# Half 0's second layer with tokens on the partitions, its norm's power ahead of weight pieces, and half 1's masks on GpSimd

## The chip, the core and the metric

The kernel runs on one core of a Trainium2 chip. In the profile PE is TensorE (PEld its weight loads), DVE is VectorE, ACT is ScalarE, POOL is GpSimd, and SP is SyncE, whose queue issues all DMAs. The metric is the device time of one execution in microseconds, the median of 3 runs.

## The reference, cut to what matters

There are 1024 tokens of 256 features. Two blocks follow each other, each with a residual. In the first, one of four experts is picked for each token by its id, and all three weights of an expert are the same matrix `ctx`:

```
e   = min(id // 3125, 3)                      # expert of each token
xn  = layernorm(x)
z   = xn @ ctx[e].T ;  h = silu(z) * z
x1  = x + h @ ctx[e].T                        # second product of the same matrices
```

The second block is a mixture of 16 experts of width 96 with a shared expert of width 96:

```
xn     = layernorm(x1)
score  = sigmoid(xn @ router.T) ; top 4 of (score + bias), weights normalised to their sum
y      = shared(xn) + sum over the 4 of weight * ((silu(xn @ gate.T) * (xn @ up.T)) @ down.T)
out    = x1 + y
```

## The kernel before, in words

Everything is in fp32. Each matrix product is made of three matmuls: every operand is split into a rounded high part and a low part (the rest), and high*high, low*high and high*low are added up in PSUM. High parts are casts, mostly by ScalarE (`high_part`, `x_high`, `hidden_high`, `hid_high`); low parts are subtractions, those of the weights by GpSimd (`low_part`), the others by VectorE.

The tokens go in two halves of 512. Data are feature-major (features on the 128 partitions, tokens along the free dimension), except for the layer norms, which want tokens on the partitions. So before a norm the tile is turned, then normalised, then turned back by TensorE (`norm_transposes`).

The first block is a list of "mixes" `(layer, half, feature half)`. `mix(n)` computes all four experts for 128 output features and 512 tokens: 24 matmuls, into four PSUM banks of a ring of six (`ring_order`, `wait_ring_read`). ScalarE copies expert 0 out (`first_z`), and VectorE overwrites it with the experts 1 to 3 where a mask says so (`pick`, masks `beyond` made by `thresholds`). `x1_transposes` turns the result of half 0 for its second norm: statistics (`tile_stats`, `layer_norm_vars`), then a power -0.5 on GpSimd (`rstd_of`), then shift and scaling (`layer_norm_apply` on VectorE, `apply_norm` on ScalarE; `BY_VECTOR` says who takes which tile).

The second block is a loop over 26 items g, each a chunk of 128 hidden features of one half: gate and up products (`gate_or_up`, 12 matmuls), silu on ScalarE, `product` with the combine weights, `hidden_2`, the split (`hid_high`, `hid_low`), and two items later the `down` product (6 matmuls). The combine weights come out of the router chain (`turn_logits`, `mark_best`, `normalise_scores`), go to DRAM (`write_rows`) and are read back spread over the partitions (`spread_rows`).

The order on each engine is written out by hand. The engines meet only in semaphores. The weights come in 15 pieces through four slots of `stage`: 0 to 3 are `ctx`, 4, 5, 8, 9, 11, 12 and 14 gate and up, 6, 7, 10 and 13 down; a slot is loaded again when both parts of its piece have been cut.

## Time and profile before

| | us |
|---|---|
| median of 3 runs | 169.52 (169.2 to 170.2) |
| the profiled execution | 169.34 |
| its span, first to last instruction | 167.2 |
| PE busy | 162.5 (97%) |
| DVE busy | 114.5 (68%) |
| ACT busy | 68.7 (41%) |
| POOL busy | 37.2 (22%) |

The granted TensorE clock was 1.00 over the whole span, which is the higher of its two levels, 2.4 GHz. A busy share is of the span. Times in the rows below are from the start of the span. In the timeline a matmul's duration (0.40 us for 512 columns) is longer than the distance to the next one, since matmuls are pipelined; the distance is what it costs.

### The profile page before, as it was taken

To read this page: it belongs to the slowest core of one execution; us is meant where nothing else is said; L and a number is where in the kernel's file an instruction comes from. 1 tells how busy PE (TensorE), PEld (TensorE's weight loads), DVE (VectorE), ACT (ScalarE), POOL (GpSimd) and SP (SyncE) were. 2 spreads that over 40 slices of the span, in tenths; PEclk is the share of its full clock that TensorE was granted. 3 is DMA by queue.
4 is the path that set the end of the run, shared out by engine and by line. 5 is a ranking of instruction groups with operands and counts; after the bars stand their busy time and mean duration, and the time that the engine had idled before them with its cause. 6 is when DMAs were issued, how large, how long until landed. Compare 5 with 4: busy or idle time off the path is not lost.

```text
span 167.2 us, 2186 instructions
## 1 busy us (share of the span) xinstructions
PE 162.5 (97%) x705; PEld 128.9 (77%) x705; DVE 114.5 (68%) x237; ACT 68.7 (41%) x116; POOL 37.2 (22%) x36
## 2 busy tenths in 40 slices
PE   7999999999999999999999999999999999999992
PEld 2788888888778888888888878888888888888880
DVE  1889999666957998779986744967714444444462
ACT  3654342831359134536734538452222222222210
POOL 1384000656241045556970000000000000000000
PEclk9999999999999999999999999999999999999999
DMA  5891380164304065987225400025441112200003
GB/s 172 275 408 44 107 291 0 21 206 161 115 4 127 16 205 192 219 240 211 67 61 163 153 0 4 1 103 165 173 141 67 63 63 63 65 0 0 4 0 125
DMA packets 12199, 18.78 MB, mean 112 GB/s; under 512 B 3772, under 2 KB 6044, under 8 KB 12060
## 3 DMA queue, kind: packets, MB, share of 16 engines
q1 hardware_dynamic: 12188, 18.64, 34.9%
q8 instruction: 6, 0.10, 0.2%
q14 instruction: 5, 0.04, 0.1%
HBM read 16.39 MB, written 2.24 MB: 111 GB/s over the span
## 4 chain that ended last, share of the span: by engine, by line
PE 95%; DMA 2%; DVE 1%; DVEq 0%; issue 0%
PE bank L1030 23%; PE bank L1131 15%; PE bank L1129 13%; PE bank L1130 13%; PE bank L1149 7%; PE bank L1152 7%; PE bank L1150 7%; DMA first<-first_d 2%; PE bank L998 1%; PE bank L1071 1%; PE bank L1065 1%; PE bank L1126 1%; PE bank L1125 1%; PE bank L987 1%; PE bank L1078 1%; PE bank L1060 1%
## 5 line engine op out<-in xcount | busy, mean ns | idle before, releaser
L1131 PE MATMUL bank<-xn_lo,gu_hi 128*128 128x512 f32 (+1 forms) x104 | 41.1, 395 | 0.0
L1129 PE MATMUL bank<-xn_hi,gu_lo 128*128 128x512 f32 x96 | 38.0, 396 | 0.0
L1130 PE MATMUL bank<-xn_hi,gu_hi 128*128 128x512 f32 x96 | 38.0, 396 | 0.0
L599 ACT ACTIVATE h_hi<-hid 128x512 fp32r<-128x512 f32 (+1 forms) x26 | 16.4, 632 | 45.6 <-DVE hid L860 45.6
L865 DVE TENSOR_TENSOR h_lo<-hid,h_hi 128x512 fp32r<-128x512 f32 (+1 forms) x26 | 18.0, 691 | 14.9 <-ACT h_hi L599 14.9
L1131 PEld LDWEIGHTS bank<-xn_lo,gu_hi 128*128 128x128 f32 (+1 forms) x104 | 19.4, 187 | 4.9
L589 ACT ACTIVATE act_sb<-bank 128x512 f32<-128x512 f32 (+1 forms) x26 | 15.4, 592 | 17.5 <-PE bank L1131 17.4
L472 POOL TENSOR_TENSOR gu_lo<-stage,gu_hi 128x512 fp32r<-128x512 f32 x12 | 17.2, 1457 | 21.7 <-ACT gu_hi L504 16.3
L1129 PEld LDWEIGHTS bank<-xn_hi,gu_lo 128*128 128x128 f32 x96 | 18.0, 188 | 4.4
L1130 PEld LDWEIGHTS bank<-xn_hi,gu_hi 128*128 128x128 f32 x96 | 18.0, 188 | 4.3
L749 DVE COPY_PREDICATED prod<-beyond,bank 128x512 f32<-128x512 uint8 x24 | 17.6, 737 | 5.1 <-PE bank L1030 4.4
L1149 PE MATMUL bank<-h_hi,wd_lo 128*128 128x512 f32 (+1 forms) x52 | 20.6, 396 | 0.0
L1150 PE MATMUL bank<-h_hi,wd_hi 128*128 128x512 f32 (+1 forms) x52 | 20.6, 395 | 0.0
L1152 PE MATMUL bank<-h_lo,wd_hi 128*128 128x512 f32 (+1 forms) x52 | 20.5, 395 | 0.0
L860 DVE TENSOR_TENSOR hid<-prod,bank 128x512 f32<-128x512 f32 x24 | 16.5, 688 | 2.0
L847 DVE TENSOR_TENSOR prod<-act_sb,ids 128x512 f32<-128x512 f32 x12 | 9.6, 796 | 8.6 <-ACT act_sb L589 8.6
L847 DVE TENSOR_TENSOR prod<-act_sb,first 128x512 f32<-128x512 f32 x12 | 10.0, 832 | 6.3 <-ACT act_sb L589 5.7
L1030 PE MATMUL bank<-h_hi,ctx_hi 128*128 128x512 f32 x32 | 12.7, 398 | 0.0
L1030 PE MATMUL bank<-h_lo,ctx_hi 128*128 128x512 f32 x32 | 12.7, 395 | 0.0
L1030 PE MATMUL bank<-h_hi,ctx_lo 128*128 128x512 f32 x32 | 12.7, 395 | 0.0
L1152 PEld LDWEIGHTS bank<-h_lo,wd_hi 128*128 128x128 f32 (+1 forms) x52 | 9.8, 188 | 2.4
L1150 PEld LDWEIGHTS bank<-h_hi,wd_hi 128*128 128x128 f32 (+1 forms) x52 | 9.8, 188 | 2.3
(102 smaller groups left out, 213.2 us busy)
## 6 DMA issues: line engine op xcount, KB each, us to landing
stage<-gu_d SPq DMA_DIRECT2D x6, 512.0 KB, 3.9
stage<-wd_d SPq DMA_DIRECT2D x3, 512.0 KB, 4.3
first<-comb_d SPq DMA_DIRECT2D x8, 192.0 KB, 2.9
ids<-comb_d SPq DMA_DIRECT2D x8, 192.0 KB, 3.3
stage<-ctx_d SPq DMA_DIRECT2D x4, 256.0 KB, 6.0
xt<-xt_d SPq DMA_DIRECT2D x1, 1024.0 KB, 9.9
first<-comb_d SPq DMA_DIRECT2D x8, 128.0 KB, 3.0
ids<-comb_d SPq DMA_DIRECT2D x8, 128.0 KB, 2.9
```

The source lines that it names most:

```text
L472: ins = nc.gpsimd.tensor_tensor(lo[:, s], st[:, s], hi[:, s].bitcast(F32), ALU.subtract)
L749: nc.vector.copy_predicated(prod[:, n % 2], beyond[:, e - 1, h * HALF:(h + 1) * HALF], ring_bank("z", n, e)[:]).then_inc(z_picked, 1)
L847: nc.vector.tensor_tensor(prod[:, g % 2], act_sb[:, g % 2], rows, ALU.mult).then_inc(prod_done, 1)
L860: nc.vector.tensor_tensor(hid[0:w, g % 2], src, up_bank(g)[0:w, :], ALU.mult).then_inc(hid_done, 1)
L865: nc.vector.tensor_tensor(h_lo[0:w, slot[g]], hid[0:w, g % 2], h_hi[0:w, slot[g]].bitcast(F32), ALU.subtract).then_inc(hlo_done, 1)
L1030: return nc.tensor.matmul(ring_bank("z", n, e)[:], (ctx_hi, ctx_lo)[a][:, m, e, k], parts[k][b], start=start, stop=stop)
L1129: nc.tensor.matmul(out[:], gu_lo[:, cols], xn_hi[:, h, k], start=(k == 0), stop=False)
L1130: nc.tensor.matmul(out[:], gu_hi[:, cols], xn_hi[:, h, k], start=False, stop=False)
L1131: ins = nc.tensor.matmul(out[0:rows, :], gu_hi[:, wide], xn_lo[:, h, k], start=False, stop=(k == KC - 1))
L1149: nc.tensor.matmul(acc[k][:], wd_lo[0:w, c, cols], hi, start=(c == 0), stop=False)
L1150: nc.tensor.matmul(acc[k][:], wd_hi[0:w, c, cols], hi, start=False, stop=False)
L1152: ins = nc.tensor.matmul(acc[k][:], wd_hi[0:w, c, cols], lo, start=False, stop=(c == ITEMS - 1))
```

## The change

In the second product of half 0, tokens and weights change places. `row_mix` takes the hidden tile h as the stationary operand, 128 tokens at a time, and the weights of two experts as the moving one (512 columns: two experts by 256 features). The result is token-major, so it needs no transposes ahead of the norm, and `x1_transposes` is gone. The picks are made per tile of 128 tokens (`row_z`, `pick_rows`, with masks `beyond_rows` from `row_thresholds`), the residual x is added from a token-major copy that is loaded into the place of half 0 in `xt` (`x_rows_d`), and the statistics read it there. Tile t holds the tokens 128 q + 32 t + i on the partitions 32 q + i; `hidden` writes h in that order, and the "n2" transposes of half 0 write it back in the natural one. Since the output needs x1 feature-major, VectorE turns it later in blocks of 32x32 (`turn_x0`, behind items 8 and 9), and SyncE writes it to DRAM and reads it back (`write_x0` and `read_x0`, at items 12 and 13). The two mixes `(2, 0, m)` leave the list; mixes 5, 6 and 7 become 3, 4 and 5.

The masks of half 1 are made by GpSimd (`late_thresholds`) behind low part 3. GpSimd's powers move too: those of the first two norms stand between low parts, that of half 0's second norm stands behind low part 5, ahead of pieces 6 and 7; these two now stand behind the wait for `xlo_done`, with piece 8. Half 1's first mix `(1, 1, 1)` is picked as a whole between the variance and the norm.

```diff
-        ring_order = [("z", n, e) for n in range(7) for e in range(E1)]
-        ring_order += [("gate", 0, 0), ("up", 0, 0)] + [("z", 7, e) for e in range(E1)]
+            count = (HALVES * KC if what == "n2" else 0) + h * KC + k + 1
+            eng.wait_ge(xhi_done, max(count, KC))
+            eng.wait_ge(xlo_done, count)
+
+        ring_order = [("z", n, e) for n in range(3) for e in range(E1)]
+        ring_order += [("rows", t, pair) for t in range(TT) for pair in range(2)]
+        ring_order += [("z", n, e) for n in (3, 4) for e in range(E1)]
+        ring_order += [("gate", 0, 0), ("up", 0, 0)] + [("z", 5, e) for e in range(E1)]
...
+            if b >= KC:
+                return tile[:, at]
+            order = "p (b t j) -> p b t j" if tile is hid else "p (t b j) -> p b t j"
+            return tile[:, at].rearrange(order, t=TT, j=LANES)
...
-        mixes = [(1, 0, 0), (1, 0, 1), (1, 1, 0), (2, 0, 0), (2, 0, 1), (1, 1, 1), (2, 1, 0), (2, 1, 1)]
+        mixes = [(1, 0, 0), (1, 0, 1), (1, 1, 0), (1, 1, 1), (2, 1, 0), (2, 1, 1)]
...
+            return x1_rows[:, t] if n == HALVES else x[:, n % HALVES * TT + t]
...
-            sp.dma_start(xt[:], xt_d).then_inc(xt_in, 16)
+            sp.dma_start(xt[:, :, HALF:], xt_d[:, :, HALF:]).then_inc(xt_in, 16)
+            sp.dma_start(id_rows[:], id_rows_d).then_inc(id_rows_in, 16)
+            sp.dma_start(xt[:, :, 0:HALF], x_rows_d).then_inc(x_rows_in, 16)
...
+            def read_x0():
+                sp.wait_ge(x0_out, QUARTERS * 16)
+                rows = turn_d.rearrange("q k i n -> q i k n")
+                for q in range(QUARTERS):
+                    sp.dma_start(xt[q * LANES:(q + 1) * LANES, :, 0:HALF], rows[q]).then_inc(x0_back, 16)
...
+            def late_thresholds():
+
+                pool.wait_ge(ids_in, 16)
+                for e in range(1, E1):
+                    nc.gpsimd.tensor_scalar(beyond[:, e - 1, HALF:], ids[:, HALF:], float(e * PER_EXPERT), None,
+                                            ALU.is_ge).then_inc(late_masked, 1)
...
-            for n in range(E1):
+            low_part(0)
+            low_part(1)
+            rstd_of(0)
+            low_part(2)
+            rstd_of(1)
+            low_part(3)
+            late_thresholds()
+            for n in range(E1, E1 + 2):
                 low_part(n)
-            rstd_of(0)
-            rstd_of(1)
-            for n in range(E1, E1 + 3):
-                low_part(n)
-            pool.wait_ge(x1_done, KC)
-            low_part(E1 + 3)
             rstd_of(2)
             pool.wait_ge(xlo_done, (HALVES + 1) * KC)
-            for n in range(E1 + 4, early_pieces + 4):
+            for n in range(E1 + 2, early_pieces + 4):
...
+            def row_z(t):
+
+                act.wait_ge(row_done, 2 * t + 1)
+                nc.scalar.activation(x1_rows[:, t], ring_bank("rows", t, 0)[:, 0:D], ACT.Copy).then_inc(row_first, 1)
...
             first_z(2)
-            first_z(3)
+            row_z(0)
             silu_z(2)
             hidden_high(2)
+            row_z(1)
             high_part(4)
             high_part(5)
+            row_z(2)
             high_part(6)
-            first_z(4)
+            row_z(3)
             high_part(7)
             high_part(8)
             router_low_rows()
-            first_z(5)
-            silu_z(5)
+            first_z(3)
+            silu_z(3)
...
+            def pick_rows(t, experts=range(1, E1)):
+
+                dve.wait_ge(row_first, t + 1)
+                dve.wait_ge(rows_masked, E1 - 1)
+                for e in experts:
+                    dve.wait_ge(row_done, 2 * t + e // 2 + 1)
+                    if e > 1:
+                        dve.wait_ge(row_picked, t * (E1 - 1) + e - 1)
+                    z = ring_bank("rows", t, e // 2)[:, e % 2 * D:(e % 2 + 1) * D]
+                    nc.vector.copy_predicated(x1_rows[:, t], beyond_rows[:, e - 1, t:t + 1].to_broadcast([P, D]),
+                                              z).then_inc(row_picked, 1)
+
+            def add_rows(t):
+
+                dve.wait_ge(row_picked, (t + 1) * (E1 - 1))
+                dve.wait_ge(x_rows_in, 16)
+                residual = xt[:, t * D // HALF, t * D % HALF:][:, 0:D]
+                nc.vector.tensor_tensor(x1_rows[:, t], x1_rows[:, t], residual, ALU.add).then_inc(row_added, 1)
+
+            def turn_x0(first):
+
+                dve.wait_ge(xn_out, QUARTERS * 16)
+                blocks = x[:, TT:].rearrange("p t d -> p (t d)").rearrange("p (q k t i) -> p t k q i", k=KC, t=TT, i=LANES)
+                for t in range(first, first + 2):
+                    for k in range(KC):
+                        ins = nc.vector.transpose(blocks[:, t, k],
+                                                  x1_rows[:, t, k * P:(k + 1) * P].rearrange("p (q i) -> p q i", i=LANES))
+                    ins.then_inc(x0_turned, 1)
...
-            masked.append(thresholds(1))
-            pick(2, masked[1])
-            pick(3, masked[0], [1])
+            row_thresholds()
+            pick(2, masked[0])
+            pick_rows(0, [1])
             hidden_product(2)
-            pick(3, masked[0], [2])
+            pick_rows(0, [2])
             hidden_low(2)
-            pick(3, masked[0], [3])
-            add_block_1(3)
-            pick(4, masked[0])
-            add_block_1(4)
-            pick(5, masked[1], [1])
-            for t in range(TT):
-                tile_stats(2, t)
+            pick_rows(0, [3])
+            add_rows(0)
+            for t in range(1, TT):
+                tile_stats(2, t - 1)
+                pick_rows(t)
+                add_rows(t)
+            tile_stats(2, TT - 1)
             layer_norm_vars(2)
-            pick(5, masked[1], [2, 3])
+            pick(3, masked[0])
             layer_norm_apply(2)
...
-            pick(6, masked[1], [1])
+            pick(4, masked[0], [1])
...
+            pick(4, masked[0], [2])
             normalise_scores(0, mark_best(0))
-            pick(6, masked[1], [3])
-            add_block_1(6)
-            pick(7, masked[1], [1])
+            pick(4, masked[0], [3])
+            add_block_1(4)
...
+                if X0_TURN <= g < X0_TURN + TT // 2:
+                    turn_x0((g - X0_TURN) * 2)
...
+                        if n == HALVES:
+                            out = banks[k][:].rearrange("p (b t j) -> p t b j", t=TT, j=LANES)[:, t]
...
+            def row_mix():
+
+                hi, lo = ([w[:, b].rearrange("p (t c) -> p t c", c=P) for b in range(KC)] for w in (h_hi, h_lo))
+
+                def moving(w, pair, k):
+                    return w[:, :, 2 * pair:2 * pair + 2, k].rearrange("p m e f -> p e m f")
+
+                for t in range(TT):
+                    for pair in range(2):
+                        wait_ring_read(pe, "rows", t, pair)
+                        out = ring_bank("rows", t, pair)[:].rearrange("p (e m f) -> p e m f", e=2, m=KC)
+                        for k in range(KC):
+                            if t == 0 and pair == 0:
+                                pe.wait_ge(h1_high, k + 1)
+                            nc.tensor.matmul(out, hi[k][:, t], moving(ctx_hi, pair, k), start=(k == 0), stop=False)
+                            nc.tensor.matmul(out, hi[k][:, t], moving(ctx_lo, pair, k), start=False, stop=False)
+                            if t == 0 and pair == 0:
+                                pe.wait_ge(h1_done, k + 1)
+                            ins = nc.tensor.matmul(out, lo[k][:, t], moving(ctx_hi, pair, k), start=False, stop=(k == KC - 1))
+                        ins.then_inc(row_done, 1)
...
-            for n in range(2, 5):
-                mix(n)
-            mix(5, {1: lambda: (x1_transposes(0, 0), x1_transposes(0, 1))})
-            mix(6, features=[0])
+            mix(2)
+            row_mix()
+            mix(3)
+            mix(4, features=[0])
             norm_transposes("n2", 2, 0)
-            mix(6, experts=[0, 1], features=[1])
+            mix(4, experts=[0, 1], features=[1])
             gate_or_up(0, False)
             gate_or_up(0, True)
-            mix(6, experts=[2, 3], features=[1])
-            mix(7)
+            mix(4, experts=[2, 3], features=[1])
+            mix(5)
```

The first place is GpSimd's order from the first low part on, to the second pair of gate-and-up pieces. `ctx_lo`, `gu_lo` and `wd_lo` are low parts of weights, `deviation` and `rstd` are powers. Before:

```order
L468 TENSOR_TENSOR ctx_lo<-stage,ctx_hi 128x512 x4
L478 TENSOR_TENSOR deviation<-vareps,power 128x4
L478 TENSOR_TENSOR rstd<-vareps,power 128x4
L468 TENSOR_TENSOR gu_lo<-stage,gu_hi 128x448
L472 TENSOR_TENSOR gu_lo<-stage,gu_hi 128x512 x2
L468 TENSOR_TENSOR wd_lo<-stage,wd_hi 96x256
L472 TENSOR_TENSOR wd_lo<-stage,wd_hi 128x512 x2
L478 TENSOR_TENSOR rstd<-vareps,power 128x4
L472 TENSOR_TENSOR gu_lo<-stage,gu_hi 128x512 x4
```

Now (`beyond` are the masks of half 1):

```order
L505 TENSOR_TENSOR ctx_lo<-stage,ctx_hi 128x512 x2
L522 TENSOR_TENSOR deviation<-vareps,power 128x4
L505 TENSOR_TENSOR ctx_lo<-stage,ctx_hi 128x512
L522 TENSOR_TENSOR rstd<-vareps,power 128x4
L505 TENSOR_TENSOR ctx_lo<-stage,ctx_hi 128x512
L516 TENSOR_SCALAR beyond<-ids 128x512 x3
L505 TENSOR_TENSOR gu_lo<-stage,gu_hi 128x448
L509 TENSOR_TENSOR gu_lo<-stage,gu_hi 128x512 x2
L522 TENSOR_TENSOR rstd<-vareps,power 128x4
L505 TENSOR_TENSOR wd_lo<-stage,wd_hi 96x256
L509 TENSOR_TENSOR wd_lo<-stage,wd_hi 128x512 x2
L509 TENSOR_TENSOR gu_lo<-stage,gu_hi 128x512 x4
```

Three compares stand behind the last `ctx_lo`, the powers `deviation` and the first `rstd` each stand one low part earlier than the end of the four, and the first down pieces (`wd_lo`, 96x256 and 128x512 x2) have moved behind the later `rstd`.

The second place is VectorE's order from the end of half 0's second product to the norm of it. `prod` and `bank` are picks of a mix, `stats`, `meanvar`, `vareps` and `shift` belong to the norm, `xn` is its result. Before:

```order
L749 COPY_PREDICATED prod<-beyond,bank 128x512
L777 TENSOR_TENSOR xt<-prod,xt 128x512
L749 COPY_PREDICATED prod<-beyond,bank 128x512 x3
L777 TENSOR_TENSOR xt<-prod,xt 128x512
L749 COPY_PREDICATED prod<-beyond,bank 128x512
L670 BN_STATS stats<-bank 128x6 x4
L676 BN_AGGR meanvar<-stats 128x2 x4
L678 TENSOR_SCALAR vareps<-meanvar 128x4
L749 COPY_PREDICATED prod<-beyond,bank 128x512 x2
L713 SCALAR_TENSOR_TENSOR shift<-meanvar,rstd 128x4
```

Now (`x_rows` is x1, token-major):

```order
L835 TENSOR_TENSOR x_rows<-x_rows,xt 128x256
L727 BN_STATS stats<-x_rows 128x6
L827 COPY_PREDICATED x_rows<-beyond_rows,bank 128x256 x3
L835 TENSOR_TENSOR x_rows<-x_rows,xt 128x256
L727 BN_STATS stats<-x_rows 128x6
L733 BN_AGGR meanvar<-stats 128x2 x4
L735 TENSOR_SCALAR vareps<-meanvar 128x4
L808 COPY_PREDICATED prod<-beyond,bank 128x512 x3
L770 SCALAR_TENSOR_TENSOR shift<-meanvar,rstd 128x4
L778 TENSOR_SCALAR xn<-x_rows,meanvar,rstd 128x256 x2
```

The statistics of a tile stand between the tiles' picks and no longer in one group behind transposes, and all three picks of the mix of half 1 stand between the variance and the shift, where there were two.

## Rows read from the trace of the kernel before

**Rows 1.** The page: busy time, share and instructions by engine; the chain by engine.
```profile
PE 162.5 (97%) x705; PEld 128.9 (77%) x705; DVE 114.5 (68%) x237; ACT 68.7 (41%) x116; POOL 37.2 (22%) x36
...
PE 95%; DMA 2%; DVE 1%; DVEq 0%; issue 0%
```

**Rows 2.** Timeline of PE from 38.9 us: start, duration, engine, line, operation, output<-input, count.
```profile
38.90 1.04 PE L1010 MATMUL bank<-first,xt 128*128 128x128 f32 x8
39.69 0.48 PE L1030 MATMUL bank<-xn_hi,ctx_hi 128*128 128x512 f32 x1
40.01 0.39 PE L1030 MATMUL bank<-xn_hi,ctx_lo 128*128 128x512 f32 x1
40.24 0.39 PE L1030 MATMUL bank<-xn_lo,ctx_hi 128*128 128x512 f32 x1
```

**Rows 3.** Timeline of PE and its weight loads, start of mix 1 and "n1" transposes.
```profile
12.61 0.19 PEld L1030 LDWEIGHTS bank<-xn_hi,ctx_hi 128*128 128x128 f32 x1
...
15.64 1.03 PE L987 MATMUL bank<-first,xn 128*128 128x128 f32 x8
```

**Rows 4.** Timeline of POOL, DVE and ACT, 8.8 to 15.9 us.
```profile
8.79 3.80 POOL L468 TENSOR_TENSOR ctx_lo<-stage,ctx_hi 128x512 fp32r<-128x512 f32 x3 [1.01 <-ACT ctx_hi L504]
9.46 0.65 DVE L678 TENSOR_SCALAR vareps<-meanvar 128x4 f32<-128x4 f32 x1
...
12.55 1.18 POOL L478 TENSOR_TENSOR deviation<-vareps,power 128x4 f32<-128x4 f32 x1
13.53 1.03 POOL L478 TENSOR_TENSOR rstd<-vareps,power 128x4 f32<-128x4 f32 x1
...
14.59 0.16 DVE L713 SCALAR_TENSOR_TENSOR shift<-meanvar,rstd 128x4 f32<-128x4 f32 x1
14.67 0.73 DVE L721 TENSOR_SCALAR xn<-first,meanvar,rstd 128x256 f32<-128x256 f32 x2
14.79 1.09 ACT L542 ACTIVATE xn<-first,shift,rstd 128x256 f32<-128x256 f32 x2 [4.30 <-DVE shift L713]
```

**Rows 5.** Timeline of POOL and DVE, the second norm of half 1.
```profile
80.67 2.55 POOL L472 TENSOR_TENSOR wd_lo<-stage,wd_hi 128x512 fp32r<-128x512 f32 x2
81.06 0.92 DVE L713 SCALAR_TENSOR_TENSOR shift<-meanvar,rstd 128x4 f32<-128x4 f32 x1
81.90 1.79 DVE L721 TENSOR_SCALAR xn<-first,meanvar,rstd 128x256 f32<-128x256 f32 x2
```

**Rows 6.** Instructions of POOL in groups; behind the bar busy us, mean ns, and idle time.
```profile
L480 POOL MEMSET comb<- 128x128 f32 x1 | 0.2, 204 | 0.1
```

**Rows 7.** Timeline of POOL, DVE and PEld: pieces 6 to 8, router chain of half 0.
```profile
34.79 0.74 POOL L468 TENSOR_TENSOR wd_lo<-stage,wd_hi 96x256 fp32r<-96x256 f32 x1
37.91 2.54 POOL L472 TENSOR_TENSOR wd_lo<-stage,wd_hi 128x512 fp32r<-128x512 f32 x2 [2.38 <-DVE xt L777]
...
48.33 2.55 POOL L472 TENSOR_TENSOR gu_lo<-stage,gu_hi 128x512 fp32r<-128x512 f32 x2 [5.38 <-DVE xn_lo L728]
50.73 0.24 DVE L800 TENSOR_TENSOR logit<-turned 128x64 f32<-128x64 f32 x1
52.11 0.21 DVE L807 TENSOR_TENSOR biased<-scores,bias 128x64 f32<-128x64 f32 x1
53.66 0.23 DVE L821 SCALAR_TENSOR_TENSOR weight<-marked,scores 128x64 f32<-128x64 f32 x1
55.09 0.70 DVE L749 COPY_PREDICATED prod<-beyond,bank 128x512 f32<-128x512 uint8 x1
55.84 0.19 PEld L1030 LDWEIGHTS bank<-h_hi,ctx_hi 128*128 128x128 f32 x1
```

**Rows 8.** Timeline of DVE and PE: variance of half 0, chunk 1 written and read.
```profile
41.69 0.17 DVE L678 TENSOR_SCALAR vareps<-meanvar 128x4 f32<-128x4 f32 x1
...
63.89 0.69 DVE L865 TENSOR_TENSOR h_lo<-hid,h_hi 128x512 fp32r<-128x512 f32 x1 [0.70 <-ACT h_hi L599]
67.21 0.40 PE L1149 MATMUL bank<-h_hi,wd_lo 128*128 128x512 f32 x1
```

More of the change, by code:

```diff
@@ L226, in wait_ring_read @@
                 eng.wait_ge(z_picked, n * (E1 - 1) + e)
+            elif what == "rows" and e == 0:
+                eng.wait_ge(row_first, n + 1)
+                eng.wait_ge(row_picked, n * (E1 - 1) + 1)
+            elif what == "rows":
+                eng.wait_ge(row_picked, (n + 1) * (E1 - 1))
         def side_bank(what, h, c):
@@ L247, in wait_features, with hidden @@
                 eng.wait_ge(side_done, side_at[what, h, k] + 1)
+        def hidden(tile, b, at):
+            if b >= KC:
+                return tile[:, at]
+            order = "p (b t j) -> p b t j" if tile is hid else "p (t b j) -> p b t j"
+            return tile[:, at].rearrange(order, t=TT, j=LANES)
         def widths(c):
@@ L422, in read_xn, with write_x0 @@
                     sp.dma_start(xn_turn[q * LANES:(q + 1) * LANES], rows[q]).then_inc(xn_back, 16)
+            def write_x0():
+                sp.wait_ge(x0_turned, TT)
+                rows = turn_d.rearrange("q k i (b c) -> b i (q k) c", c=P)
+                blocks = x[:, TT:].rearrange("p t d -> p (t d)").rearrange("p (m c) -> p m c", c=P)
+                for b in range(QUARTERS):
+                    sp.dma_start(rows[b], blocks[b * LANES:(b + 1) * LANES]).then_inc(x0_out, 16)
+            def read_x0():
[3 more added lines that the diff above has]
+                    sp.dma_start(xt[q * LANES:(q + 1) * LANES, :, 0:HALF], rows[q]).then_inc(x0_back, 16)
             def spread_rows(g):
@@ L450, in _ @@
                     read_xn()
+                if g == X0_WRITE:
+                    write_x0()
+                if g == X0_READ:
+                    read_x0()
                 if g == place[1, SPREADS]:
@@ L546, in hidden_high @@
                 act.wait_ge(h1_product, b + 1)
-                nc.scalar.activation(h_hi[:, b], hid[:, b % 2], ACT.Copy).then_inc(h1_high, 1)
+                nc.scalar.activation(hidden(h_hi, b, b), hidden(hid, b, b % 2), ACT.Copy).then_inc(h1_high, 1)
             def router_low_rows():
@@ L750, in pick, with row_thresholds @@
                                               ring_bank("z", n, e)[:]).then_inc(z_picked, 1)
+            def row_thresholds():
+                dve.wait_ge(id_rows_in, 16)
+                for e in range(1, E1):
+                    nc.vector.tensor_scalar(beyond_rows[:, e - 1], id_rows[:], float(e * PER_EXPERT), None,
+                                            ALU.is_ge).then_inc(rows_masked, 1)
+            def pick_rows(t, experts=range(1, E1)):
[21 more added lines that the diff above has]
+                    ins.then_inc(x0_turned, 1)
             def hidden_product(n):
@@ L762, in hidden_cast @@
                 dve.wait_ge(h1_product, b + 1)
-                nc.vector.tensor_scalar(h_hi[:, b], hid[:, b % 2], 1.0, None, ALU.mult).then_inc(h1_high, 1)
+                nc.vector.tensor_scalar(hidden(h_hi, b, b), hidden(hid, b, b % 2), 1.0, None, ALU.mult).then_inc(h1_high, 1)
             def hidden_low(n):
@@ L986, in norm_transposes @@
                     for k in range(KC):
-                        ins = nc.tensor.transpose(banks[k][:, t * P:(t + 1) * P], xn[:, t, k * P:(k + 1) * P],
-                                                  consts_sb[:, 0:P])
+                        out = banks[k][:, t * P:(t + 1) * P]
+                        if n == HALVES:
+                            out = banks[k][:].rearrange("p (b t j) -> p t b j", t=TT, j=LANES)[:, t]
+                        ins = nc.tensor.transpose(out, xn[:, t, k * P:(k + 1) * P], consts_sb[:, 0:P])
                         if t == TT - 1:
@@ L1001, in first_transposes @@
                         ins.then_inc(first_turned, 1)
-            def x1_transposes(h, pair):
-                pe.wait_ge(x1_done, (h + 1) * KC)
-                b = side_wait("x1", h, pair)
-                for t in range(TT // KC):
-                    at = h * HALF + (pair * (TT // KC) + t) * P
-                    for k in range(KC):
-                        ins = nc.tensor.transpose(b[:, t * D + k * P:t * D + (k + 1) * P], xt[:, k, at:at + P],
-                                                  consts_sb[:, 0:P])
-                ins.then_inc(side_done, 1)
+            def row_mix():
[15 more added lines that the diff above has]
+                        ins.then_inc(row_done, 1)
             def mix(n, between={}, experts=range(E1), features=range(KC)):
```

66 lines of the change are left out of this document (38 added, 28 removed).

## The prediction

> **What bounds the kernel now.** I read the page's busy times and its chain first: TensorE is busy for 97% of the span and holds 95% of the chain that ended last [rows 1]. So only what TensorE executes, or waits for, can move the time. The timeline of TensorE then shows how full it is: behind the first transposes one 512-column matmul starts every 0.233 us (40.01 to 40.24), and no matmul group of the page has idle time before it. What is left to win lies in work that TensorE need not do; anything that makes it wait is lost for good, since there is no later gap to make it up. The other engines matter only through their distance to TensorE, so I looked next for the places where that distance is small, and for what VectorE and GpSimd do there.
>
> **What the change takes off TensorE.** The matmul count stays: two mixes of 24 become 48 matmuls of `row_mix`, and I price them alike. The eight transposes of `x1_transposes` go. They run from 38.90 to 39.69, and the matmul behind them needs 0.32 us to its successor in place of 0.233 [rows 2]: 0.79 + 0.09 = 0.88 us. The eight "n2" transposes stay. **Term 1: -0.88 us.** Two forms are not in the trace: weights as the moving operand in four runs of 128 columns, and a transpose written in runs of 32. From below they cost nothing (a matmul row is 0.233 us per 512 columns); from above, at the transposes' rate of about 0.1 us for 128 columns, four runs would be 0.4 us, or 48 x 0.17 = 8 us. I take 0: a transpose is short and pays its fixed part each time, a run inside one matmul does not.
>
> **The GpSimd compares land on the first norm of half 1.** Before, GpSimd makes three low parts from 8.79 at 1.27 us each, then the two powers, 0.98 us apart, and is idle from 14.56 [rows 4]. Now the first power goes behind low part 1: it waits for the variance, which ended at 9.46 + 0.65 = 10.11; low part 2 then runs about 11.15 to 12.42, the second power from 12.7, low part 3 from 13.70 to 14.97, and the compares behind it from 15.02. TensorE loads its first weights of mix 1 at 12.61 [rows 3], so low part 2 is 0.2 us early: no cost, though this cover is thin.
>
> What VectorE does there is what counts: the shift at 14.59, then two tiles of the norm in 0.73 us, with ScalarE starting its two at 14.79, as the shift ends [rows 4]. GpSimd is idle at that moment before. The same three instructions in the second norm of half 1 show what happens when it isn't: the shift takes 0.92 us, ending as GpSimd's first half of 2.55 us ends (80.67 + 1.27 = 81.94), and the two tiles take 1.79 us, because GpSimd's second half has slipped in and holds them to 83.2 [rows 5]. VectorE and GpSimd take turns there, each waiting for the other's whole instruction. The variance at 9.46, 0.65 us for four numbers, waited for low part 1 in the same way [rows 4].
>
> So in the new order: the shift waits for low part 3 (14.97, done 15.06); compare 1 begins; the tile of t=0 waits for it; compare 2 gets the next turn; the tile of t=2 waits for that. A compare of 512 is not in the trace. From below stands the memset of 128 elements at 0.20 us [rows 6]: 0.8 us for 512 if all of it grows with the elements, about 0.5 if half of it is fixed; from above the 1.27 us of a two-input subtract of 512 (2.54 for two) [rows 7]. I take 0.9 us, about the middle, as it reads one stream where the subtract reads two. A tile is 0.35 us of its own. Then t=0 is done at 15.02 + 0.9 + 0.35 = 16.27, and t=2 at 16.27 + 0.9 + 0.35 = 17.52. TensorE transposes in the order 0, 1, 2, 3, from 15.64 at about 0.1 us each, so t=2 began at 16.05 [rows 3]; now its load begins at 17.55 and its matmul at about 17.75. **Term 2: +1.70 us** (0.9 for a compare of 0.5 us, 2.45 for one of 1.27). ScalarE's tiles slip by 0.3 us only and are not last. The compares are over near 18.4, and their first reader, a pick of half 1, stands behind all hidden products of half 0. That VectorE no longer makes them saves nothing on TensorE.
>
> The Trainium skill, page "SBUF — State Buffer", section "Who interferes with whom", has this as an exclusive pair of ports that the later instruction waits for in full, when VectorE reads SBUF twice or runs a `tensor_scalar` on two ports; the rows agree (0.92 us for a 0.16 us shift). The skill's "GPSIMD Engine Reference", section 3.1, gives 769 ns for a tight loop over 512 elements; by that estimate term 2 would be 1.45 us instead. No run here shows it.
>
> **The row stage.** Behind mix 2 VectorE has, for each tile, three picks of 256, an addition and the statistics, and TensorE 12 matmuls of 0.233 = 2.8 us. A pick of 512 takes 0.70 us [rows 7]; at about 0.45 for each of the five passes of 256 that is 2.25 us: it keeps up, and half of a mix is left behind it. So its variance is ready about 2 us before the 41.69 + 0.17 of before [rows 8], so the power's new place costs nothing and gains nothing: the norm is applied behind the last pick of mix (1,1,1), which TensorE releases, both before and after. I price it at 0, with up to 1 us if the strided forms are slow. The new loads, `turn_x0` (about 2 us of VectorE over two chunks) and its eight DMAs come where VectorE idles in each chunk and SyncE waits for half 1's weights: 0.
>
> **Weight pieces moved onto the router chain.** Pieces 6 and 7 used to be cut at 34.79 (0.74 us) and 37.91 (2.54 us) [rows 7]. Now they stand behind the wait for `xlo_done`, in front of piece 8, which starts at 48.33. In before's clock, GpSimd is then busy from 48.33 to 49.05, 51.60 and 54.2, in steps of 1.27, and not idle from 50.88. VectorE's sum of logits (two SBUF inputs, 50.73) waits to 51.60; the pick behind it has room. The biased scores would start at 52.3 and wait for the first half of piece 8, which the sum has pushed to 51.72 to 52.99: done near 53.09, where it was 52.11 + 0.21 = 52.32. The weights (53.66) then come at 54.43, just after GpSimd ends. So the chain is 0.77 us late, and behind it stands the pick of expert 3, 55.09 to 55.79, for which TensorE's bank waits: its weight load started at 55.84, a few hundredths late already [rows 7]. There is no slack at all. **Term 3: +0.75 us** (0 if the turns fall well; 1.5 if a further step of the chain waits for a half piece).
>
> Behind it, the DMAs of pieces 10 to 12 come just before the combine rows and can delay the first chunk's product by about a microsecond; the low part of chunk 1 is written from 63.89 and read at 67.21 [rows 8], so 2.6 us of cover: 0.
>
> **Sum.** -0.88 + 1.70 + 0.75 = +1.57 us. The profiled execution took 169.34 us (span 167.2 and 2.1 around it), 0.18 under the median of 169.52. It becomes 170.9, the median 171.1; I take 171.0.
>
> **The rivals.** (A) VectorE keeps the turn for both tiles once it has it: t=0 done at 16.27, t=2 at 16.6, and TensorE starts its transposes at about 16.5 where it was 15.64: term 2 is 0.85, the sum +0.7, the time 170.2 us. For it: the trace has no place with two such VectorE instructions behind each other while GpSimd waits. Against: between GpSimd's two halves at 81.9 VectorE did get its turn, so the waiting engine goes first. (B) Ends on the other side: the compare does not hold VectorE at all, and the router chain meets gaps. Then term 1 stands alone: 168.6 us. It decides at the point where the compares are over by the time the shift has run, or need no turn; against it is [rows 5]. With term 3 still there it is 169.4. (C) The compare is a slow one, 1.3 us or more, or the strided matmuls or the row stage cost some tenths: 172 to 173 us. (D) The change doesn't do what it says, in that the row stage is late and the norm waits for it: the same side as C.
>
> **How the numbers follow.** Forecast 48%, A 18%, B 18% (8 of them with term 1 alone, 10 with term 3 still there), C and D 16%. What a measurement can tell from no change is 0.5%, 0.85 us: 168.67 to 170.37. Faster is B's first part: 0.08. Same is the rest of B (0.10), most of A (0.14) and the forecast with a compare under 0.6 us (0.10): 0.34. Slower is what is left: 0.38 + 0.04 + 0.16 = 0.58. The range 168.9 to 172.2 leaves out B's 0.08 and the half of C and D that is above 172.2; the forecast's own range is 170.4 to 171.7.
>
> **What would show it.** Term 1: no transposes from `xt`, and matmuls 0.233 us apart in the row stage; a wider spacing would be the strided operand. Term 2: VectorE's two norm tiles near 15 to 17.5 taking over 2 us in all, and TensorE idle between its "n1" transposes; if they take 0.73 us, term 2 is wrong. Term 3: two-input VectorE instructions of the router chain at 0.8 us or more beside GpSimd's pieces, and a TensorE gap before the last expert of the last mix. The forecast is wrong if TensorE has no gap between 15 and 20 us, or has one in the row stage.

## The result, and the profile after

The changed kernel takes 171.49 us (median of 10 runs, 170.41 to 173.12), the kernel before 169.69 us on the same chip (10 runs, 169.08 to 170.20). The ratio is 1.011, 95% interval 1.0084 to 1.0137: slower, as forecast (171.0, range 168.9 to 172.2). Its profiled execution took 171.16 us, span 168.7; before's 169.34, span 167.2. The profiles differ by 1.5 us in span, and the forecast's sum was 1.57. The number is right, and by luck: two of the three terms behind it are wrong by 1.7 us each, in opposite directions.

The page of the changed kernel, busy times and chain, against [rows 1]:

```profile
PE 161.7 (96%) x697; PEld 127.1 (75%) x697; DVE 121.0 (72%) x253; ACT 69.0 (41%) x118; POOL 41.6 (25%) x39
...
PE 88%; DVE 3%; DMA 3%; issue 2%; ACT 1%; POOL 1%; SPq 0%; DVEq 0%; POOLq 0%
```

TensorE is busy 0.8 us less and has eight instructions less (697, not 705), yet the span is longer: its share of the chain fell from 95% to 88%. It waits somewhere now.

**Term 1, the transposes.** The timeline of TensorE in the row stage, and where the "n2" transposes follow:

```profile
28.33 0.40 PE L1118 MATMUL bank<-ctx_hi,h_hi 128*128 128x512 f32 x1
28.56 0.39 PE L1119 MATMUL bank<-ctx_lo,h_hi 128*128 128x512 f32 x1
28.79 0.40 PE L1122 MATMUL bank<-ctx_hi,h_lo 128*128 128x512 f32 x1
...
44.42 1.03 PE L1089 MATMUL bank<-first,xn 128*128 128x128 f32 x8
45.21 0.48 PE L1141 MATMUL bank<-h_hi,ctx_hi 128*128 128x512 f32 x1
```

The strided matmuls start 0.23 us apart like all others, and no transposes read `xt`. Before, the first matmul behind the "n2" transposes started at 46.16; it starts at 45.21 now: -0.95, of which 0.09 is an earlier start (mix 1 begins at 12.75, before at 12.84). That leaves -0.86, forecast -0.88. The "n2" transposes themselves, written in runs of 32, take 0.79 us to the next matmul, as in [rows 2].

**Term 2, the compares.** POOL, DVE, ACT and PE at the first norm of half 1, against [rows 3, 4]:

```profile
13.54 1.29 POOL L505 TENSOR_TENSOR ctx_lo<-stage,ctx_hi 128x512 fp32r<-128x512 f32 x1
14.91 3.19 POOL L516 TENSOR_SCALAR beyond<-ids 128x512 uint8<-128x512 int32 x2
...
14.09 0.75 DVE L770 SCALAR_TENSOR_TENSOR shift<-meanvar,rstd 128x4 f32<-128x4 f32 x1
14.76 1.02 DVE L778 TENSOR_SCALAR xn<-first,meanvar,rstd 128x256 f32<-128x256 f32 x2
...
14.88 1.10 ACT L594 ACTIVATE xn<-first,shift,rstd 128x256 f32<-128x256 f32 x2 [4.59 <-DVE shift L770]
...
15.55 1.04 PE L1089 MATMUL bank<-first,xn 128*128 128x128 f32 x8
```

A compare takes about 1.5 us (1.49 at the median, 1.62 the first), more than the upper bound of 1.27 in the prediction. But VectorE's two tiles take 1.02 us together (0.73 before), not the 2.5 of the forecast, and TensorE runs its eight transposes without a gap. The cost is 0 in place of 1.70.

**Term 3, the router chain.** POOL, DVE, ACT and PE, against [rows 7]:

```profile
47.38 0.74 POOL L505 TENSOR_TENSOR wd_lo<-stage,wd_hi 96x256 fp32r<-96x256 f32 x1 [6.04 <-DVE xn_lo L785]
48.08 2.53 POOL L509 TENSOR_TENSOR wd_lo<-stage,wd_hi 128x512 fp32r<-128x512 f32 x2
50.57 2.54 POOL L509 TENSOR_TENSOR gu_lo<-stage,gu_hi 128x512 fp32r<-128x512 f32 x2
...
49.78 3.41 DVE L895 TENSOR_TENSOR logit<-turned 128x64 f32<-128x64 f32 x1
53.11 0.72 DVE L808 COPY_PREDICATED prod<-beyond,bank 128x512 f32<-128x512 uint8 x1
53.74 0.20 DVE L902 TENSOR_TENSOR biased<-scores,bias 128x64 f32<-128x64 f32 x1
...
53.23 0.26 ACT L621 ACTIVATE scores<-logit 128x64 f32<-128x64 f32 x1 [2.52 <-DVE logit L895]
...
57.44 0.50 PE L1141 MATMUL bank<-h_hi,ctx_hi 128*128 128x512 f32 x1 [1.88 <-DVE prod L808]
```

GpSimd cuts pieces 6, 7 and 8 in five subtracts without a pause, 47.38 to 53.11. VectorE's sum of logits is due at 49.78, in the middle of the third subtract. It does not come in at the boundary behind that one (50.6), nor at the next (near 51.8), but only when the whole run is over: 3.41 us for an instruction of 0.24. (Two of the expectations below say that it missed three boundaries; it is two, and the third is the end of the run.) TensorE's matmul before the gap started at 55.16, the next at 57.44: 2.28 where 0.233 is usual, so 2.05 lost, with 0.22 more at an earlier pick (53.44 to 53.89) and 0.11 behind each of the two waits, where the first matmul needs 0.34 to its successor. Together 2.49 us, forecast 0.75. The chain, -0.86 - 0.09 + 2.49 = +1.54, is the difference of the two profiles: the second chunk's first gate matmul starts at 58.94, before at 57.41.

### The profile page after: what moved, and what is told of

It is laid out like the page before. It is cut to its first block, busy times and chain, and to the rows that moved or that the text cites. A ratio compares the mean times of both kernels' runs of the same rounds, so it can differ in the third digit from the quotient of the medians.

```text
span 168.7 us, 2210 instructions
## 1 busy us (share of the span) xinstructions
PE 161.7 (96%) x697; PEld 127.1 (75%) x697; DVE 121.0 (72%) x253; ACT 69.0 (41%) x118; POOL 41.6 (25%) x39
## 4 chain that ended last, share of the span: by engine, by line
PE 88%; DVE 3%; DMA 3%; issue 2%; ACT 1%; POOL 1%; SPq 0%; DVEq 0%; POOLq 0%
PE bank L1242 14%; PE bank L1141 13%; PE bank L1241 13%; PE bank L1240 13%; PE bank L1260 7%; PE bank L1263 7%; PE bank L1261 7%; DMA stage<-ctx_d 3%; PE bank L1118 2%; PE bank L1122 2%; PE bank L1119 2%; PE bank L1176 1%; PE bank L1182 1%; PE bank L1089 1%; DVE prod L808 1%
## 5 line engine op out<-in xcount | busy, mean ns | idle before, releaser
L808 DVE COPY_PREDICATED prod<-beyond,bank 128x512 f32<-128x512 uint8 x18 | 13.1, 731 | 0.6
L1260 PEld LDWEIGHTS bank<-h_hi,wd_lo 128*128 128x128 f32 (+1 forms) x52 | 9.8, 188 | 2.4
L1141 PE MATMUL bank<-xn_hi,ctx_hi 128*128 128x512 f32 x24 | 9.6, 399 | 0.0
L1141 PE MATMUL bank<-xn_lo,ctx_hi 128*128 128x512 f32 x24 | 9.5, 396 | 0.0
```

The source lines that it names most:

```text
L1141: return nc.tensor.matmul(ring_bank("z", n, e)[:], (ctx_hi, ctx_lo)[a][:, m, e, k], parts[k][b], start=start, stop=stop)
L1260: nc.tensor.matmul(acc[k][:], wd_lo[0:w, c, cols], hi, start=(c == 0), stop=False)
```

## The experiments

In the lines of edits, `...` stands for text left out. Two theories stood at the start. **S**: the loss is that uninterrupted run of subtracts, and nothing of the row stage or its DMAs. **R**: the token-major layer brings its own loss. A third, **M**, was that the masks on GpSimd cost something at the first norm. Each run was timed beside the kernel before, whose medians were 169.25 to 169.44 in all of them.

**Pieces 6 and 7 put back in front of the wait.** In the changed kernel:

```
-            for n in range(E1, E1 + 2):
+            for n in range(E1, E1 + 4):
                 low_part(n)
             rstd_of(2)
             pool.wait_ge(xlo_done, (HALVES + 1) * KC)
-            for n in range(E1 + 2, early_pieces + 4):
+            for n in range(E1 + 4, early_pieces + 4):
```

> The changed kernel with weight pieces 6 and 7 cut where they were, ahead of the power of half 0's second norm. Theory S (the loss is GpSimd's uninterrupted run of pieces 6, 7 and 8, which holds VectorE's sum of logits for 3.4 us and TensorE for 2.05 + 0.2 us plus two slow restarts): both TensorE gaps go, the span falls by about 2.4 us to 166.3, the time to 168.7 to 169.1, ratio to before 0.995 to 0.998. Theory R (token-major form or new DMAs cost TensorE): the gaps stay or move, 170 or more. Theory M (the compares on GpSimd cost in some executions): the spread of 2.7 us between executions stays, the median lies near 169.5.

**Half 1's masks back on VectorE.** `late_thresholds` and its waits go, `masked.append(thresholds(1))` stands behind `row_thresholds`.

> The changed kernel with half 1's masks made by VectorE again, in front of its first pick of half 1; pieces 6 and 7 stay late. Theory S: no change of the median, about 171.2; the gap of 2 us before the last expert stays. Theory M (compares collide with the first norm of half 1 in some executions): the executions above 171.5 vanish, the median falls by 0.3 to 0.7 us and the spread with it.

**Both of these.**

> Both of the above: pieces 6 and 7 early and the masks on VectorE; what is left of the change is the token-major layer, the powers' new places and the turn of x1. Theory S: equal to the first of these runs within 0.3 us, near 168.8, which is the 0.88 us of the eight transposes under before. Theory M: 0.3 to 0.7 us under the first. Theory R: 170 or more.

**The kernel before, with its pieces 6 and 7 moved behind the wait for `xlo_done`**, and nothing of the row stage:

```
-            for n in range(E1, E1 + 3):
+            for n in range(E1, E1 + 2):
                 low_part(n)
-            pool.wait_ge(x1_done, KC)
-            low_part(E1 + 3)
             rstd_of(2)
             pool.wait_ge(xlo_done, (HALVES + 1) * KC)
-            for n in range(E1 + 4, early_pieces + 4):
+            for n in range(E1 + 2, early_pieces + 4):
                 low_part(n)
```

> The kernel before with one part of the change alone: pieces 6 and 7 cut behind the wait for xlo_done, in front of piece 8, and the power of half 0 ahead of them. Theory S: slower than before by 2 to 2.6 us (172), with one TensorE gap of about 2 us before the last expert of the last mix and VectorE's sum of logits at over 3 us. If VectorE gets its turn at each piece boundary, as the prediction had it, slower by 0.75 us. Theory R: within 0.3 us of before.

| run | median us (range) | ratio to before, 95% | gap before the last experts |
|---|---|---|---|
| pieces back | 169.22 (168.71 to 170.34) | 0.999, 0.9964 to 1.0015 | none |
| masks on VectorE | 171.50 (171.10 to 173.62) | 1.0144, 1.0091 to 1.0198 | 55.95 to 58.23 |
| both | 169.11 (168.83 to 169.86) | 0.9982, 0.996 to 1.0003 | none |
| before, pieces late | 172.32 (171.87 to 173.32) | 1.0174, 1.0131 to 1.0216 | 56.17 to 58.46 |

S holds from both sides: without the late pieces the whole loss against the kernel before goes, and with them alone that kernel loses 1.7%. That is more than the changed one's 1.1%, as it should be without term 1's 0.88 us, though the intervals just touch (1.0131 and 1.0137). R, as worded, falls: neither run without the late pieces takes 170 us. Where the masks are made moves no median that these runs can tell apart. In the kernel before with late pieces, the sum is held as in the changed kernel, across the same boundaries:

```profile
50.79 3.42 DVE L798 TENSOR_TENSOR logit<-turned 128x64 f32<-128x64 f32 x1
54.13 0.72 DVE L747 COPY_PREDICATED prod<-beyond,bank 128x512 f32<-128x512 uint8 x1
```

But with the pieces back, 0.88 us should have been won. The medians are 0.1 to 0.2% under before, which their intervals don't tell from nothing; both lie above what was expected. In the profile of "pieces back" low part 3 (14.60 to 15.89) holds the shift, and TensorE's distance at the first norm is 0.74 in place of 0.233. In the changed kernel's profile the shift was held as long, but 1.1 us earlier, and that cost nothing.

```profile
15.15 0.75 DVE L770 SCALAR_TENSOR_TENSOR shift<-meanvar,rstd 128x4 f32<-128x4 f32 x1
15.83 1.02 DVE L778 TENSOR_SCALAR xn<-first,meanvar,rstd 128x256 f32<-128x256 f32 x2
```

**The powers in before's order too**, from "both": low parts 0 to 3, then the two powers. (In the change the first power stands two low parts earlier than before and the second one, not one each as said ahead of the prediction.)

> From `e3_both` (pieces 6 and 7 in front of the wait again, half 1's masks by VectorE) with the first two powers put behind low part 3 as well, as in the kernel before. Theory P: what was left of the 0.88 us in `e1_pieces_back` and `e3_both` went to the interleaving of powers and low parts, which lets low part 3 hold the shift (0.75 us in place of 0.16) and opens a TensorE gap of 0.5 to 0.6 us at the first norm of half 1. Then the shift takes 0.2 us or less, that gap is gone, and the time is 168.5 to 168.7, against 169.1 of `e3_both`. Rival Q: the gap there is set by the tiles' arrival or by ScalarE's tiles and stays when the powers go back: 169.1.

169.19 us (median of nine runs, 168.72 to 170.89; its profiled execution, a tenth, took 906 us and tells nothing), ratio 1.0001 (0.9973 to 1.0028). Against "both" (0.9982) nothing is won that can be measured; the expected time was missed.

**The three compares directly behind the powers**, and VectorE no longer makes these masks; otherwise the same. It is the purest form of what term 2 priced.

```
             rstd_of(0)
             rstd_of(1)
+            late_thresholds()
```

> `e5_powers_back` with the three compares of half 1 on GpSimd, directly behind its two powers, so that they start as VectorE's shift does and nothing else of GpSimd's is there. The prediction's mechanism for term 2: VectorE's two tiles wait for one compare each (a compare of 1.5 us), tiles of 2.5 us or more in place of 0.73, a TensorE gap of over 2 us, 171 us or more. Rival: the compares do not hold VectorE's tensor_scalar tiles, they only stretch them a little (1.0 us for both), no gap, and the time is that of `e5_powers_back` within 0.2 us.

169.19 us (168.11 to 169.78), ratio 0.9982 (0.9963 to 1.0002): the rival. Here compare 1 starts as the shift does, and the tiles are stretched by 0.3 us, not held. One by one they take 0.73 and 0.40 us, in the changed kernel 0.40 and 0.70: in both it is the tile that starts next behind the first compare's start.

```profile
14.17 4.67 POOL L516 TENSOR_SCALAR beyond<-ids 128x512 uint8<-128x512 int32 x3
...
14.12 0.16 DVE L768 SCALAR_TENSOR_TENSOR shift<-meanvar,rstd 128x4 f32<-128x4 f32 x1
14.20 1.05 DVE L776 TENSOR_SCALAR xn<-first,meanvar,rstd 128x256 f32<-128x256 f32 x2
```

The same profile answers what the run before it could not: with the powers in before's order the shift is 0.16 us again and the gap is gone; its span is 166.4.

**Three two-input subtracts in the compares' place**, results not used:

```
+            for n in range(3):
+                nc.gpsimd.tensor_tensor(spare[:, n], ids[:, 0:HALF].bitcast(F32),
+                                        ids[:, HALF:].bitcast(F32), ALU.subtract)
```

> `e5_powers_back`, with three extra subtracts of 512 elements (two inputs in SBUF, results not used) on GpSimd where `e6_masks_at_the_norm` had its three compares. Theory V: what holds VectorE's two norm tiles is a two-input GpSimd instruction, not a compare; then the mechanism that term 2 assumed shows here: the tiles take 1.8 us or more in place of 0.73 (2.5 if each waits for a subtract, 3.8 if they miss the boundaries as the sum of logits did), TensorE has a gap of 1 us or more behind 16 us, and the time is 170 to 171.5. Rival W: no GpSimd instruction holds these tiles, and their 1.79 us in the second norm has another cause: tiles near 1 us, no gap, 169.2.

172.83 us (171.87 to 173.38), ratio 1.0199 (1.0163 to 1.0235): theory V, and slower than it expected, since the profile shows a second gap (46.09 to 47.28) that no theory named. It is the second norm: one addition of the row stage took 1.43 us in place of 0.42, and the tiles came late. At the first norm it shows what term 2 had described:

```profile
13.84 3.80 POOL L534 TENSOR_TENSOR spare<-ids 128x512 f32<-128x512 f32 x3
...
14.41 0.74 DVE L772 SCALAR_TENSOR_TENSOR shift<-meanvar,rstd 128x4 f32<-128x4 f32 x1
15.08 2.71 DVE L780 TENSOR_SCALAR xn<-first,meanvar,rstd 128x256 f32<-128x256 f32 x2
...
16.66 0.63 PE L1090 MATMUL bank<-first,xn 128*128 128x128 f32 x4 [0.97 <-DVE xn L780]
```

The two tiles take 1.35 and 1.44 us, one subtract each, in turns. So the mechanism exists, but the compare does not set it off. The two differ in inputs (one against two), in operation and in types (int32 to uint8 against fp32), and which of these decides was not tested.

**GpSimd pausing between its subtracts.** In the changed kernel, for pieces 6 to 8, GpSimd waits for its own last subtract before it issues the next:

```
                     ins = nc.gpsimd.tensor_tensor(lo[:, s], st[:, s], ...)
+                    if n in (E1 + 2, E1 + 3, E1 + 4) and part == 0:
+                        ins.then_inc(half_low, 1)
+                        halves[0] += 1
+                        pool.wait_ge(half_low, halves[0])
                 ins.then_inc(w_lo, 1)
+                if n in (E1 + 2, E1 + 3, E1 + 4):
+                    pool.wait_ge(w_lo, n + 1)
```

> The changed kernel, where GpSimd waits for its own last subtract at each boundary of pieces 6, 7 and 8, so that the next one is not queued behind it back to back. Theory T: VectorE's sum of logits missed three boundaries only because GpSimd's next subtract stood ready; with a wait between them it comes in at the first one, takes 0.9 to 1.5 us, and TensorE's gap before the last experts shrinks by 1.5 us or so: 169.8 to 170.2. Rival U: the sum needs GpSimd to be through with the whole run, whatever stands between: 3.4 us still, 171.5 us or more.

169.25 us (169.02 to 170.36), ratio 0.9999 (0.9981 to 1.0016): theory T, and more than it expected. Each set against before on its own chip, this kernel is at -0.2 us and the changed one at +1.8, so the pauses give back 2.0. The pieces stay in their late place and take 0.4 us longer from the first start to the last end (6.1 for 5.7):

```profile
47.66 0.74 POOL L508 TENSOR_TENSOR wd_lo<-stage,wd_hi 96x256 fp32r<-96x256 f32 x1 [5.93 <-DVE xn_lo L794]
48.36 2.65 POOL L512 TENSOR_TENSOR wd_lo<-stage,wd_hi 128x512 fp32r<-128x512 f32 x2
51.09 2.67 POOL L512 TENSOR_TENSOR gu_lo<-stage,gu_hi 128x512 fp32r<-128x512 f32 x2
...
50.05 1.04 DVE L904 TENSOR_TENSOR logit<-turned 128x64 f32<-128x64 f32 x1
51.02 0.74 DVE L817 COPY_PREDICATED prod<-beyond,bank 128x512 f32<-128x512 uint8 x1
51.65 0.82 DVE L911 TENSOR_TENSOR biased<-scores,bias 128x64 f32<-128x64 f32 x1
...
55.98 0.50 PE L1150 MATMUL bank<-h_hi,ctx_hi 128*128 128x512 f32 x1 [0.48 <-DVE prod L817]
```

The sum comes in at the first boundary, the biased scores wait once more for half a piece. TensorE's matmul before the gap is at 55.11, so the gap costs 0.64, and 0.11 behind it: 0.75 us. That is term 3 as the prediction described it, step for step.

**What keeps the sum out.** Two runs on the changed kernel: the sum as a `scalar_tensor_tensor`, and an extra four-element one, the norm's shift once more, ahead of it.

> The changed kernel with the sum of logits as a scalar_tensor_tensor (times 1, plus the low part) in place of a tensor_tensor. The shift of the second norm of half 1, a scalar_tensor_tensor, came in at the first boundary between two GpSimd subtracts (0.92 us), while the sum missed three (3.41 us). Theory F: the form decides; in this form the sum takes 1.5 us or less, the gap before the last experts shrinks, 170.0 to 170.4. Rival G: any two-input instruction misses the boundaries of this run: 3.4 us still, 171.5.

> The changed kernel with one more scalar_tensor_tensor of four elements (the same as the shift of the norm, result not used) on VectorE, directly ahead of the sum of logits. Open is why the shift and the norm's tiles come in at the next boundary between two GpSimd subtracts and the sum of logits does not. Theory K: it lies in the sum itself (64 elements in strided blocks): then the small one comes in at the first boundary (under 1 us) and the sum behind it is held to the end of the run. Rival L: it lies in the place, in this run of GpSimd's: then the small one is held for 3.4 us as the sum was, the sum behind it takes 0.24 us, and the time stays 171 to 172.8.

The other form took 172.75 us (172.33 to 173.12) and its sum 3.44: form does not decide. The small one took 3.37 us, and the sum behind it 0.21, at 171.36 us (170.82 to 171.81):

```profile
50.84 3.37 DVE L895 SCALAR_TENSOR_TENSOR spare<-meanvar,rstd 128x4 f32<-128x4 f32 x1
54.13 0.21 DVE L899 TENSOR_TENSOR logit<-turned 128x64 f32<-128x64 f32 x1
```

Rival L: it lies in the place, not in the instruction. Yet at the norm with three extra subtracts, which also had no pause between them, VectorE had its turns. What makes this run different stays open; that a pause ends it is shown.

**The last two.** From "powers in before's order", the six products of mix (2,1,0) behind the "n2" transposes take h_hi four times, then h_lo twice; in the profile of "both", a weight load had waited 0.43 us there for h_lo. On TensorE that cost less, 0.26 us: the matmuls are 0.38 apart, and 0.34 behind it, where 0.233 is usual. The second adds the masks on GpSimd.

```
+                if split:
+                    operands(1, False)
+                    for e in experts:
+                        term(e, 1, 0, 0)
+                        term(e, 1, 1, 0)
+                    operands(1, True)
+                    for e in experts:
+                        term(e, 1, 0, 1, stop=True).then_inc(z_done, 1)
+                    return
```

> `e5_powers_back`, and behind the transposes of the second norm the six products of mix (2,1,0) over the second block with h_hi come ahead of those with h_lo for both experts (four, then two), since TensorE waited 0.43 us there for h_lo, two products after it had begun. If that gap, with the slow restart behind it, is as real a loss as the others, 0.5 us go: 168.0 to 168.2. If h_lo then comes in as late for another reason, or the time before is fixed by the ending, it stays at the time of `e5_powers_back`.

> Both of what won or cost nothing: `e6_masks_at_the_norm` (half 1's masks on GpSimd behind the powers in before's order, pieces 6 and 7 early) with the six split products of `e8_products_split`. If VectorE's time freed by the masks is worth nothing to TensorE, as in `e6_masks_at_the_norm` against `e5_powers_back`, this is 168.8 like `e8_products_split`; if it is worth something, 168.4 to 168.6.

168.82 us (168.63 to 169.78), ratio 0.9965 (0.9944 to 0.9987), and 168.74 us (168.42 to 169.31), ratio 0.9968 (0.9952 to 0.9984). The first missed the expected 168.0 to 168.2, the second met its 168.8. Both are faster than either kernel, by 0.3% than before, and so by 1.4% than the changed one (1.011 against 0.997). In their profiles no two matmuls start more than 0.35 us apart between 12 us and the end. Whether the split did it is not settled: the three compared on one chip read 169.19, 169.19 and 168.82, but the profile of the second showed no wait for h_lo either.

**Where the rest of the 0.88 us went.** The profile of "compares directly behind the powers" has all of it: from the "n1" transposes to the last matmul 147.01 us (15.77 to 162.78), before 147.89 (15.64 to 163.53). That of the last version has half: 147.45. There the eight "n2" transposes take 1.19 us to the next matmul (44.28 to 45.47), not 0.79:

```profile
36.11 1.57 DVE L833 TENSOR_TENSOR x_rows<-x_rows,xt 128x256 f32<-128x256 f32 x1
...
44.13 1.08 ACT L592 ACTIVATE xn<-x_rows,shift,rstd 128x256 f32<-128x256 f32 x2
...
44.28 1.42 PE L1087 MATMUL bank<-first,xn 128*128 128x128 f32 x8
```

GpSimd's subtracts of piece 7, which run from 36.10, held one of VectorE's additions for 1.57 us (0.42 alone), the norm came later, and ScalarE's tiles end at 45.21, when TensorE is already in its transposes. The same shows in the profile, where there is a usable one, of every version of the changed kernel with pieces 6 and 7 early or half 1's masks on VectorE, but for the first of these two: from the first "n2" transpose to the last 1.06 to 1.16 us (1.36 with the three subtracts), in place of 0.76. So a loss of R's kind exists, 0.3 to 0.4 us set against the 0.88 won, as soon as something takes VectorE about 1 us in the row stage. This is read from profiles of single executions; no run was made for it.

## Why the prediction was right in the number and wrong in two steps

**The bound**, TensorE with no slack to make up a wait, was right: every gap found in a profile is in its span. **Term 1** was right in both sizes: -0.86 for -0.88, and nothing for the strided operand. In the best version it shows as -0.54 us of median (168.74 against 169.28), less than the term; the late second norm above is about the size of the rest.

**Term 2 failed, in its mechanism.** The step was "the shift waits for low part 3; compare 1 begins; the tile of t=0 waits for it". The first part happened (0.75 us), the rest did not. The prediction took a compare for one more instruction like the subtract of [rows 5]. The nearest row in kind was missing, and the prediction said so, but it bounded only the compare's length from both sides and not whether it holds VectorE at all; that stood only as rival B. By the prediction's own sign it was wrong: TensorE has no gap between 15 and 20 us. The Trainium skill, page "SBUF — State Buffer", section "Who interferes with whom", lets whichever of a two-port `tensor_scalar` and GpSimd issues first hold the other for its whole instruction. The trace agrees for GpSimd's two-input subtract (2.71 us for both tiles) and not for its compare (1.05 us). ScalarE's tiles, said to slip by 0.3 us, slipped by 0.09.

**Term 3 was right in its place and mechanism and mis-sized.** It named the late pieces, the sum of logits, the biased scores and the pick before the last expert, and priced 0.75 us. Where GpSimd pauses between subtracts, 0.75 us is what is measured. Without the pause it is 2.49, outside its own upper end of 1.5. The failed step is "VectorE's sum of logits waits to 51.60", which assumed that VectorE gets its turn at the next boundary. [Rows 5] showed one such turn, and one was taken for a rule. The errors, -1.70 and +1.74, add up to 0.04: that the sum came out right is luck.

**The row stage and DMAs** cost nothing on TensorE in this kernel, as priced: it has no gap from 16.7 to 44.4 us. VectorE is nearer to it than forecast, though, and in the experiments that took more of its time there the second norm was late, as shown above. Its variance is ready at 40.06 + 0.17, 1.6 us before the old time and not 2, and GpSimd's pieces 4 and 5 stretch two of its four additions there to 1.14 and 0.73 us, from 0.42.

**The rivals.** A and C fell with term 2 (no cost at the norm); the slow compare of C was real and harmless. B's first half was right, that the compare does not hold VectorE. Its second, that the router chain meets gaps (168.6), was the opposite of what happened. Its other end (169.4, term 3 still there) had the structure right and failed by the size of term 3, 1.74 us.

## What to carry to other kernels

Before moving GpSimd work to a later place, look at what stands behind it: a piece of 0.7 us and one of 2.5 us that had cost the kernel before nothing became costly when they closed up with a third into one run of 5.7 us across a chain of short VectorE steps. Either leave the run broken up, or let GpSimd wait for its own last instruction between the parts; here that cost 0.4 us of GpSimd and gave back 2.0 us. And when a sum comes out right, compare each term with its own place in the trace: this one hid two errors of 1.7 us.

## What the runs showed of the hardware that was not expected

- A VectorE instruction of 0.2 us with two inputs in SBUF took 3.14 to 3.44 us, past two boundaries of a run of GpSimd subtracts, in five kernels and in two forms. With a pause at the boundaries it took 1.04.
- A GpSimd compare of 512 elements from int32 to uint8 took 1.49 us, longer than a two-input subtract of as many (1.27). It did not hold VectorE's `tensor_scalar` tiles, but stretched one of the two from 0.40 to 0.70 us.
- A moving operand in four strided runs of 128 columns costs a matmul nothing (0.233 us apart).
- A gap of TensorE of 2.3 us can cost more than itself, and need not. In the profile of "sum in another form" the granted clock is 1.00 in the gap and 0.97 just behind it, and then 0.50 for 3 us, the 1.2 GHz level: matmuls start 0.427 us apart, not 0.233.

```profile
55.10:57.40 2.30, 0.40 (x3) 0.01 (x1) 2.04 (x8) 0.72 (x2) 0.00 (x0) 1.00 0.40 162
57.40:58.69 1.29, 1.29 (x6) 1.04 (x7) 1.25 (x3) 0.00 (x0) 0.00 (x0) 0.97 0.15 43
58.69:61.67 2.98, 2.98 (x8) 2.34 (x7) 2.77 (x6) 0.63 (x1) 0.00 (x0) 0.50 0.30 95
```

The columns are the stretch and its length, the busy time of PE, PEld, DVE, ACT and POOL, the granted clock, the DMA share and GB/s. Of the ten runs of the changed kernel, the four with a mean clock of 0.99 took 172.13 to 173.12 us, the six at 1.00 took 170.41 to 171.82. Of "sum in another form" all four runs are at 0.99, of the extra small instruction, with the same gap, all four at 1.00. The changed versions without a gap of 1 us or more have no run under 0.996; of the kernel before's 80 runs with a clock on record two are at 0.987 (171.2 us) and one at 0.66 (231.72 us). So the fall of the clock is the likely reason that the changed kernel scatters over 2.7 us, and of a part of the 2.0 us that the pauses gave back. What decides in which executions it falls stays open.
